# A deformable convolution's sampling weights: two pairs of row positions copied out of PSUM in one operation instead of two

## The chip, the core and the metric

The kernel runs on one core of one Trainium2 chip. The time is device microseconds of the whole program, the median of several runs.

## What is computed

The input `x` is 4 images of 128 channels and 32 x 32 pixels. Two residual blocks follow each other. The first holds nearly all of the instructions that matter here: a 3 x 3 convolution gives, for each pixel and each of nine taps, an offset in y, an offset in x and a mask; each tap reads the image at its shifted, fractional place (four neighbours, bilinear weights), and a 1 x 1 product over taps and channels gives the output.

```python
x = x + L0(group_norm(x))     # deformable 3x3 convolution, bias, group norm of 16 groups
x = x + L1(group_norm(x))     # two ternary 3x3 convolutions with batch norm
...
om = conv2d(x, w_off, b_off)                  # 27 channels
off_y, off_x, m = split(om, 3); mask = sigmoid(m)
py = base_y + kgy + off_y;  px = base_x + kgx + off_x
sampled = sum over 4 corners of x[corner] * wy * wx * valid
sampled = sampled * mask
out = einsum("bckhw,ock->bohw", sampled, weight) + bias
```

## The kernel before

Sampling is done as a matrix product. For a pair of image rows and a half of the columns, the pixels that any tap can reach lie in a window of 6 x 19 = 114 positions. A matrix with 114 rows (positions) and one column for each tap and pixel holds the sampling weights, and TensorE multiplies the window's pixels (`patch`) by it. Products in TensorE's `float32r` form lose low bits, so each operand is split into a high part (`shi`, a rounded copy) and a low part (`slo`, source minus high part).

The work runs over 36 chunks, nine to an image. A chunk n covers two pairs of rows, u = 0 and u = 1, and the ninth of an image only one (`pairs(n)` is 2 in 32 chunks and 1 in 4). The path of the weights of one chunk is:

- GpSimd makes the weights of 128 pixels with the pixels on the partitions (`vt`, L503).
- TensorE turns them: `turn_pairs_out` (L664) writes 16 small transposes, eight taps for each pair, into `S_PAIR[0]` and `S_PAIR[1]`, which are the first two PSUM banks, 114 x 512 numbers each. `turn_last_out` (L673) writes the ninth tap of both pairs into a third bank, `S_LAST`.
- ScalarE copies them to `shi`: `weights_hi`, one copy for each pair (L962) and one for the ninth tap (L966).
- VectorE makes `slo`: `weights_lo`, one subtraction for each pair (L1316), and one for the ninth tap (L1319).
- TensorE samples (`sample`, L693 to L695), into a PSUM area that ScalarE (`vhi`, L974) and VectorE (`vlo`, L1327) empty, and `combine` (L711 to L713) multiplies by the convolution's weights. ScalarE's `output` (L981) empties that.

Each engine runs its own list in a fixed order written by hand, in slots. In slot n TensorE does `sample(n, 0)`, a piece of `combine`, `sample(n, 1)`, then waits for `slo_ok` to reach 3n + 6 (all low parts of chunk n + 1), then does a small job `beside(n)` where there is one, `turn_pairs_out(n + 2)`, another piece and `turn_last_out(n + 2)`. The jobs beside are sums of a normalisation (L552, L557), steps that make the ternary weights (L723, L726, L734) and one test of the offsets (L718). In its slot ScalarE does `sampled_hi(n, 0)`, the hat functions of chunk n + 4 (L953, L955), `output`, `sampled_hi(n, 1)`, `weights_hi(n + 2)` and its own `beside(n)`. VectorE does `sampled_lo(n, 0)`, `sampled_lo(n, 1)`, `weights_lo(n + 2)` and its `beside(n)` (statistics among them, L1216 and L1224). The semaphores `s_mm`, `shi_ok` and `slo_ok` rise by three for each chunk. `turn_pairs_out(n)` also waits for 3n - 1 of `slo_ok`, since it writes over the banks that `weights_lo(n - 1)` reads.

Of the kernel before, what the change touches and what calls it, by code (L numbers as in the profile page):

```python
# [8 lines left out]
ALU = mybir.AluOpType  # L9
ACT = mybir.ActivationFunctionType  # L10
# [3 lines left out]
P = 128  # L14
# [13 lines left out]
KW = WR * WC  # L28
# [25 lines left out]
def build(nc, x, w_off, b_off, wd, bias, gamma, beta, w1, g1, be1, w2, g2, be2, out):  # L54
# [8 lines left out]
    with ExitStack() as ctx:  # L63
        def sb(name, shape, dt=F32, of=None):
            return (of or ctx).enter_context(nc.sbuf_tensor(name, shape, dt))

        def sem(name):
            return ctx.enter_context(nc.semaphore(name))
# [51 lines left out]
        with ExitStack() as own:  # L120
            shi = sb("shi", [KW, 2, TAPS * P], F32R, own)
            slo = sb("slo", [KW, 2, TAPS * P], F32R, own)
# [27 lines left out]
        PS = ctx.enter_context(nc.psum_tensor("PS", [P, 2 * B, BIG], F32))  # L150
# [1 line left out]
        OM_PS = [PS[:, 4 + m, 0:4 * STACK].rearrange("p (j y c) -> p j y c", j=4, y=K) for m in range(4)]  # L152
        T_PS = [PS[:, 2 * m:2 * m + 2, :].rearrange("p a (k c) -> p (a k) c", c=P) for m in range(2)]

        S_PAIR = [PS[0:KW, u, :].rearrange("p (t n) -> p t n", n=P // 2) for u in range(2)]
        S_LAST = PS[0:KW, 2, 0:P]
        WD_PS = [PS[:, m, 0:K * P] for m in (6, 2, 3)]
        V_PS = [PS[:, 3 + 2 * u:5 + 2 * u, 0:2 * TAPS * HALF] for u in range(2)]
# [26 lines left out]
        s_mm, shi_ok, slo_ok = sem("s_mm"), sem("shi_ok"), sem("slo_ok")  # L185
# [74 lines left out]
        def pairs(n):  # L260
            return 1 if n % CH == CH - 1 else 2
# [4 lines left out]
        def pairs_through(n):  # L266
            return pair_no(n, pairs(n) - 1) + 1
# [5 lines left out]
        def taps_at(n, u):  # L273

            s = 4 * (n % CH) + 2 * u
            return (K, TAPS) if s == 0 else (0, 2 * K) if s == H else (0, TAPS)

        def by_pair(m, n):

            return m[:, n % 2, :].rearrange("k (u t p) -> k u t p", u=2, t=TAPS)  # L280

        def first_taps(n):
            return min(TAPS - 1, taps_at(n, pairs(n) - 1)[1])
# [248 lines left out]
        def _(pe):  # L532
# [121 lines left out]
            def turn_pairs_out(n):  # L654
# [6 lines left out]
                for tap in range(first_taps(n)):  # L661
                    for u in range(pairs(n)):
                        at = slice(u * P // 2, (u + 1) * P // 2)
                        ins = t.transpose(S_PAIR[u][:, tap, :], vt[at, n % 2, tap, :], ident[at, at])  # L664
                        if tap == first_taps(n) - 1:
# [220 lines left out]
        def _(act):  # L886
            a = nc.scalar
# [69 lines left out]
            def weights_hi(n):  # L957
                act.wait_ge(s_mm, 3 * n + pairs(n) + (pairs(n) == 1) * 2)
                if n >= 2:
                    act.wait_ge(v_mm, pairs_through(n - 2))  # L960
                for u in range(pairs(n)):
                    a.activation(by_pair(shi, n)[:, u, 0:first_taps(n), :], S_PAIR[u][:, 0:first_taps(n), :],  # L962
                                 ACT.Copy).then_inc(shi_ok, 1 if pairs(n) == 2 else 3)
                if pairs(n) == 2:
                    act.wait_ge(s_mm, 3 * n + 3)
                    a.activation(by_pair(shi, n)[:, :, TAPS - 1, :], S_LAST.rearrange("k (u p) -> k u p", u=2),  # L966
                                 ACT.Copy).then_inc(shi_ok, 1)
# [41 lines left out]
            def slot(n):  # L1009
                if n >= 0:  # L1010
                    sampled_hi(n, 0)
                if n + 4 < CHUNKS:
                    hats(n + 4)
                if ends_in(n):
                    output(*ends_in(n))
                if n in TURNS:
                    copy_weights(TURNS.index(n))
                if n >= 0:
                    sampled_hi(n, 1)
                if n + 2 < CHUNKS:  # L1020
                    weights_hi(n + 2)
                beside(n)
# [125 lines left out]
        def _(dve):  # L1148
            d = nc.vector
# [160 lines left out]
                d.tensor_scalar(fari[0:1, 0:1], far[0:1, B + 1:B + 2], float(REACH), None, ALU.is_le).then_inc(far_ok, 1)  # L1310

            def weights_lo(n):
                for u in range(pairs(n)):
                    dve.wait_ge(shi_ok, 3 * n + (u + 1 if pairs(n) == 2 else 3))
                    src, hi, lo = (m[:, 0:first_taps(n), :] for m in (S_PAIR[u], by_pair(shi, n)[:, u, :, :], by_pair(slo, n)[:, u, :, :]))
                    d.tensor_tensor(lo, src, hi, ALU.subtract).then_inc(slo_ok, 1 if pairs(n) == 2 else 3)  # L1316
                if pairs(n) == 2:
                    dve.wait_ge(shi_ok, 3 * n + 3)
                    d.tensor_tensor(by_pair(slo, n)[:, :, TAPS - 1, :], S_LAST.rearrange("k (u p) -> k u p", u=2),  # L1319
                                    by_pair(shi, n)[:, :, TAPS - 1, :], ALU.subtract).then_inc(slo_ok, 1)  # L1320
# [43 lines left out]
            def slot(n):  # L1364
                if n >= 0:
                    sampled_lo(n, 0)
                    sums_read(n)
                    sampled_lo(n, 1)
                if n + 2 < CHUNKS:
                    weights_lo(n + 2)  # L1370
                beside(n)
# [138 lines left out]
            with dve.Else():  # L1510
# [34 lines left out]
                for b in range(B):  # L1545
# [3 lines left out]
                    with dve.Fori(0, TAPS) as k:  # L1549
# [27 lines left out]
                        for pt in range(NT):  # L1577
                            for half in range(2):
                                n = (it * NT + pt) * 2 + half
# [50 lines left out]
```

## Time and profile before

| | us |
|---|---|
| median of 3 runs (lowest to highest) | 288.46 (288.09 to 289.36) |
| the profiled execution's own time | 288.8 |
| its span, first to last instruction | 287.0 |
| chunks' part of the span | about 38 to 192 |
| PE busy / weight loads busy | 251.6 / 217.6 |
| DVE busy | 193.4 |
| ACT busy | 171.0 |

PE is TensorE, DVE is VectorE, ACT is ScalarE, POOL is GpSimd. The part from 192 us on is the second block's two convolutions, which the change doesn't touch.

### The profile page before, as it was taken

The numbers are of one execution on the slowest core, as the hardware profiler recorded it, in microseconds if no ns is written. First come the engines' busy times: TensorE is split into PE (matmuls) and PEld (weight loads), VectorE is DVE, ScalarE is ACT, GpSimd is POOL, SyncE is SP. The second block draws the span as 40 slices with busy tenths as digits, with TensorE's granted clock in tenths as the row PEclk, the third lists the DMA queues.
The fourth block names the chain that finished last, engine by engine and source line by source line (L and its number), as shares of the span: only waits on it lengthen the run. The fifth ranks groups of instructions, "written<-read, shape, count | busy, mean of one in ns | idle before, by whom it ended". The sixth has DMA issues, their size and how long they took to land.

```text
span 287.0 us, 5560 instructions
## 1 busy us (share of the span) xinstructions
PE 251.6 (88%) x1980; PEld 217.6 (76%) x1980; DVE 193.4 (67%) x450; ACT 171.0 (60%) x366; POOL 136.7 (48%) x193
## 2 busy tenths in 40 slices
PE   2699999999899999989989999999989959999900
PEld 2577667899798899889988889988867737777600
DVE  5689556989888995689977899771365353115194
ACT  2488675888679878788898778830044024330061
POOL 9300799999659688956769875140000000000040
PEclk9999997999999999999999999999999997999965
DMA  7915676544443323333323343000000000000016
GB/s 230 360 36 184 212 256 233 158 134 135 138 136 115 119 64 106 123 95 115 98 83 103 127 129 101 20 2 0 0 0 2 0 0 0 0 3 0 5 40 257
DMA packets 25737, 28.13 MB, mean 98 GB/s; under 512 B 2525, under 2 KB 23629, under 8 KB 25704
## 3 DMA queue, kind: packets, MB, share of 16 engines
q1 hardware_dynamic: 25200, 26.47, 28.1%
q10 hardware_dynamic: 504, 1.24, 1.3%
q8 instruction: 18, 0.29, 0.4%
q14 instruction: 15, 0.12, 0.1%
HBM read 19.87 MB, written 6.78 MB: 93 GB/s over the span
## 4 chain that ended last, share of the span: by engine, by line
PE 65%; DVE 17%; ACT 8%; issue 3%; DMA 3%; POOL 1%; SPq 1%; POOLq 0%; DVEq 0%
PE PS L797 23%; PE PS L711 6%; PE PS L664 5%; PE PS L712 5%; PE PS L713 5%; PE PS L693 5%; PE PS L695 4%; PE PS L694 4%; DVE slo L1316 4%; PE PS L593 3%; ACT vhi L974 3%; DVE vlo L1327 2%; DVE xb L1419 2%; DVE st L1216 2%; ACT shi L962 1%
## 5 line engine op out<-in xcount | busy, mean ns | idle before, releaser
L503 POOL TENSOR_TENSOR vt<-rowm,hat 128x1026 f32<-128x1026 f32 x36 | 70.8, 1966 | 26.0 <-PE PS L673 24.6
L1327 DVE TENSOR_TENSOR vlo<-PS,vhi 128x576 fp32r<-128x576 f32 (+2 forms) x88 | 49.9, 588 | 17.1 <-ACT vhi L974 16.8
L974 ACT ACTIVATE vhi<-PS 128x576 fp32r<-128x576 f32 (+2 forms) x88 | 43.8, 523 | 18.9 <-PE PS L695 18.7
L1316 DVE TENSOR_TENSOR slo<-PS,shi 114x512 fp32r<-114x512 f32 (+1 forms) x68 | 43.2, 674 | 6.4 <-ACT shi L962 6.1
L711 PE MATMUL PS<-vhi,wdhi 128*128 128x256 f32 x144 | 43.8, 304 | 1.8 <-ACT xb L981 1.8
L529 POOL TENSOR_TENSOR xb<-xb,xs 128x512 f32<-128x512 f32 x3 | 3.7, 1278 | 86.0 <-ACT xb L1049 86.0
L693 PE MATMUL PS<-shi,patch 114*128 114x288 f32 (+1 forms) x136 | 43.4, 319 | 0.5 <-DVE omr L1472 0.3
L797 PE MATMUL PS<-xhi,q 128*128 128x512 f32 (+1 forms) x144 | 38.4, 412 | 3.4 <-ACT xhi L1044 3.4
L695 PE MATMUL PS<-shi,patch 114*128 114x288 f32 (+1 forms) x136 | 40.9, 301 | 0.0
L694 PE MATMUL PS<-slo,patch 114*128 114x288 f32 (+1 forms) x136 | 40.8, 300 | 0.0
L713 PE MATMUL PS<-vhi,wdlo 128*128 128x256 f32 x144 | 40.5, 282 | 0.0
L712 PE MATMUL PS<-vlo,wdhi 128*128 128x256 f32 x144 | 40.5, 281 | 0.0
L962 ACT ACTIVATE shi<-PS 114x512 fp32r<-114x512 f32 (+1 forms) x68 | 36.7, 592 | 4.2 <-PE PS L664 3.7
L797 PE MATMUL PS<-xlo,q 128*128 128x512 f32 (+1 forms) x144 | 37.9, 409 | 0.0
L797 PEld LDWEIGHTS PS<-xhi,q 128*128 128x128 f32 x144 | 27.5, 193 | 10.7 <-ACT xhi L1044 3.8
L797 PEld LDWEIGHTS PS<-xlo,q 128*128 128x128 f32 x144 | 27.7, 195 | 6.8
L711 PEld LDWEIGHTS PS<-vhi,wdhi 128*128 128x128 f32 x144 | 27.2, 189 | 4.0 <-issue 1.3
L693 PEld LDWEIGHTS PS<-shi,patch 114*128 114x128 f32 x136 | 26.3, 194 | 1.7 <-issue 1.6
L712 PEld LDWEIGHTS PS<-vlo,wdhi 128*128 128x128 f32 x144 | 27.3, 190 | 0.1
L713 PEld LDWEIGHTS PS<-vhi,wdlo 128*128 128x128 f32 x144 | 27.1, 188 | 0.0
L694 PEld LDWEIGHTS PS<-slo,patch 114*128 114x128 f32 x136 | 26.5, 195 | 0.1
L695 PEld LDWEIGHTS PS<-shi,patch 114*128 114x128 f32 x136 | 26.3, 194 | 0.0
(158 smaller groups left out, 430.9 us busy)
## 6 DMA issues: line engine op xcount, KB each, us to landing
patch<-xt SPq DMA_DIRECT2D x136, 114.0 KB
xt<-xtt SPq DMA_DIRECT2D x4, 1024.0 KB, 6.1
xs<-in_x SPq DMA_DIRECT2D x3, 512.0 KB, 7.7
out<-xb SPq DMA_DIRECT2D x6, 256.0 KB, 2.3
wraw<-in_L_conv_w SPq DMA_DIRECT2D x2, 576.0 KB, 9.8
wd_raw<-in_L_conv_weight ACTq DMA_DIRECT2D x1, 576.0 KB, 6.9
xs<-in_x SPq DMA_DIRECT2D x2, 256.0 KB, 3.9
omr<-omr SPq DMA_DIRECT2D x8, 64.0 KB, 4.1
```

The lines of the kernel that those rows point to most:

```text
L503: g.tensor_tensor(vt[:, n % 2, :, :].rearrange("p t (r j) -> p t r j", r=WR), rowm[:, n % 2, :, :].unsqueeze(3).to_broadcast([P, TAPS, WR, ...
L693: t.matmul(v, patch[:, n % PATCHES, m, 0, :], hi[at], start=True, stop=False)
L694: t.matmul(v, patch[:, n % PATCHES, m, 0, :], lo[at], start=False, stop=False)
L695: last = t.matmul(v, patch[:, n % PATCHES, m, 1, :], hi[at], start=False, stop=True)
L711: t.matmul(O_PS, wdhi[:, w, :], hi, start=(tap == TAPS - 1), stop=False)
L712: t.matmul(O_PS, wdhi[:, w, :], lo, start=False, stop=False)
L713: last = t.matmul(O_PS, wdlo[:, w, :], hi, start=False, stop=(tap == 0))
L797: last = t.matmul(tap_out(PS[:, 2 * b + h, :], h, k), q[:, k, :], tap_in(src, b, h, k), start=(i == 0 and part == 0), stop=(i == TAPS - 1 ...
L962: a.activation(by_pair(shi, n)[:, u, 0:first_taps(n), :], S_PAIR[u][:, 0:first_taps(n), :], ACT.Copy).then_inc(shi_ok, 1 if pairs(n) == 2 ...
L974: last = a.activation(places(vhi), src, ACT.Copy)
L1316: d.tensor_tensor(lo, src, hi, ALU.subtract).then_inc(slo_ok, 1 if pairs(n) == 2 else 3)
L1327: last = d.tensor_tensor(places(vlo), src, places(vhi), ALU.subtract)
```

## The change

The two PSUM banks get one name, `S_PAIRS`, with the pair as a dimension; `S_PAIR[u]` is now a slice of it. `weights_hi(n)` issues one copy over both banks, and `weights_lo(n)` one subtraction over both, with one wait that asks for the whole copy. The counts of the semaphores after each step are as before. The ninth tap's two operations stay, and so do the four chunks with one pair, whose single operation over one bank is the same as before.

```diff
--- before.py
+++ after.py
@@ -152,7 +152,8 @@
         OM_PS = [PS[:, 4 + m, 0:4 * STACK].rearrange("p (j y c) -> p j y c", j=4, y=K) for m in range(4)]
         T_PS = [PS[:, 2 * m:2 * m + 2, :].rearrange("p a (k c) -> p (a k) c", c=P) for m in range(2)]
 
-        S_PAIR = [PS[0:KW, u, :].rearrange("p (t n) -> p t n", n=P // 2) for u in range(2)]
+        S_PAIRS = PS[0:KW, 0:2, :].rearrange("p u (t n) -> p u t n", n=P // 2)
+        S_PAIR = [S_PAIRS[:, u, :, :] for u in range(2)]
         S_LAST = PS[0:KW, 2, 0:P]
         WD_PS = [PS[:, m, 0:K * P] for m in (6, 2, 3)]
         V_PS = [PS[:, 3 + 2 * u:5 + 2 * u, 0:2 * TAPS * HALF] for u in range(2)]
@@ -958,9 +959,8 @@
                 act.wait_ge(s_mm, 3 * n + pairs(n) + (pairs(n) == 1) * 2)
                 if n >= 2:
                     act.wait_ge(v_mm, pairs_through(n - 2))
-                for u in range(pairs(n)):
-                    a.activation(by_pair(shi, n)[:, u, 0:first_taps(n), :], S_PAIR[u][:, 0:first_taps(n), :],
-                                 ACT.Copy).then_inc(shi_ok, 1 if pairs(n) == 2 else 3)
+                a.activation(by_pair(shi, n)[:, 0:pairs(n), 0:first_taps(n), :], S_PAIRS[:, 0:pairs(n), 0:first_taps(n), :],
+                             ACT.Copy).then_inc(shi_ok, 2 if pairs(n) == 2 else 3)
                 if pairs(n) == 2:
                     act.wait_ge(s_mm, 3 * n + 3)
                     a.activation(by_pair(shi, n)[:, :, TAPS - 1, :], S_LAST.rearrange("k (u p) -> k u p", u=2),
@@ -1310,10 +1310,9 @@
                 d.tensor_scalar(fari[0:1, 0:1], far[0:1, B + 1:B + 2], float(REACH), None, ALU.is_le).then_inc(far_ok, 1)
 
             def weights_lo(n):
-                for u in range(pairs(n)):
-                    dve.wait_ge(shi_ok, 3 * n + (u + 1 if pairs(n) == 2 else 3))
-                    src, hi, lo = (m[:, 0:first_taps(n), :] for m in (S_PAIR[u], by_pair(shi, n)[:, u, :, :], by_pair(slo, n)[:, u, :, :]))
-                    d.tensor_tensor(lo, src, hi, ALU.subtract).then_inc(slo_ok, 1 if pairs(n) == 2 else 3)
+                dve.wait_ge(shi_ok, 3 * n + (2 if pairs(n) == 2 else 3))
+                src, hi, lo = (m[:, 0:pairs(n), 0:first_taps(n), :] for m in (S_PAIRS, by_pair(shi, n), by_pair(slo, n)))
+                d.tensor_tensor(lo, src, hi, ALU.subtract).then_inc(slo_ok, 2 if pairs(n) == 2 else 3)
                 if pairs(n) == 2:
                     dve.wait_ge(shi_ok, 3 * n + 3)
                     d.tensor_tensor(by_pair(slo, n)[:, :, TAPS - 1, :], S_LAST.rearrange("k (u p) -> k u p", u=2),
```

ScalarE's list in slot 3, which is `sampled_hi(3, 0)`, the hat functions of chunk 7, `sampled_hi(3, 1)` and `weights_hi(5)`, and the first operation of slot 4, before:

```order
L974 ACTIVATE vhi<-PS 128x2x18x16
L953 ACTIVATE hat<-hat 128x225
L955 ACTIVATE hat<-hat 128x225
L974 ACTIVATE vhi<-PS 128x2x18x16
L962 ACTIVATE shi<-PS 114x512 x2
L966 ACTIVATE shi<-PS 114x2x64
L974 ACTIVATE vhi<-PS 128x2x6x16
```

and now:

```order
L974 ACTIVATE vhi<-PS 128x2x18x16
L954 ACTIVATE hat<-hat 128x225
L956 ACTIVATE hat<-hat 128x225
L974 ACTIVATE vhi<-PS 128x2x18x16
L962 ACTIVATE shi<-PS 114x2x512
L966 ACTIVATE shi<-PS 114x2x64
L974 ACTIVATE vhi<-PS 128x2x6x16
```

Two copies of 114 x 512 became one of 114 x 2 x 512, at the same place in the list; in the changed kernel the hat functions' lines are numbered one higher.

VectorE's list from `weights_lo(2)` to `weights_lo(3)`, with `sampled_lo(1, ...)` between them and the test of the offsets (`far`), before:

```order
L1316 TENSOR_TENSOR slo<-PS,shi 114x512 x2
L1319 TENSOR_TENSOR slo<-PS,shi 114x2x64
L1327 TENSOR_TENSOR vlo<-PS,vhi 128x2x18x16
L1309 TENSOR_REDUCE far<-PS 1x1
L1310 TENSOR_SCALAR fari<-far 1x1
L1327 TENSOR_TENSOR vlo<-PS,vhi 128x2x18x16
L1316 TENSOR_TENSOR slo<-PS,shi 114x512 x2
L1319 TENSOR_TENSOR slo<-PS,shi 114x2x64
```

and now:

```order
L1315 TENSOR_TENSOR slo<-PS,shi 114x2x512
L1318 TENSOR_TENSOR slo<-PS,shi 114x2x64
L1326 TENSOR_TENSOR vlo<-PS,vhi 128x2x18x16
L1309 TENSOR_REDUCE far<-PS 1x1
L1310 TENSOR_SCALAR fari<-far 1x1
L1326 TENSOR_TENSOR vlo<-PS,vhi 128x2x18x16
L1315 TENSOR_TENSOR slo<-PS,shi 114x2x512
L1318 TENSOR_TENSOR slo<-PS,shi 114x2x64
```

Here, too, two operations became one in place and nothing changed its neighbour. TensorE's list holds the same instructions in the same order.

## Rows read from the trace of the kernel before

**Rows 1.** The page's busy times, and its chain that ended last, by engine and line.

```profile
PE 251.6 (88%) x1980; PEld 217.6 (76%) x1980; DVE 193.4 (67%) x450; ACT 171.0 (60%) x366; POOL 136.7 (48%) x193
...
PE 65%; DVE 17%; ACT 8%; issue 3%; DMA 3%; POOL 1%; SPq 1%; POOLq 0%; DVEq 0%
PE PS L797 23%; PE PS L711 6%; PE PS L664 5%; PE PS L712 5%; PE PS L713 5%; PE PS L693 5%; PE PS L695 4%; PE PS L694 4%; DVE slo L1316 4%; PE PS L593 3%; ACT vhi L974 3%; DVE vlo L1327 2%; DVE xb L1419 2%; DVE st L1216 2%; ACT shi L962 1%
```

**Rows 2.** Instructions by line and form: line, operation, tiles, count | busy, mean ns | idle before.

```profile
L1316 DVE TENSOR_TENSOR slo<-PS,shi 114x512 fp32r<-114x512 f32 x64 | 41.0, 682 | 6.4 <-ACT shi L962 6.1
...
L962 ACT ACTIVATE shi<-PS 114x512 fp32r<-114x512 f32 x64 | 34.8, 599 | 4.2 <-PE PS L664 3.7
...
L1467 DVE TENSOR_TENSOR xtt<-PS,xtt 128x1024 fp32r<-128x1024 f32 x4 | 4.9, 1222 | 3.3 <-ACT xtt L943 3.2
...
L943 ACT ACTIVATE xtt<-PS 128x1024 fp32r<-128x1024 f32 x4 | 4.1, 1014 | 0.0
```

**Rows 3.** Timeline of ScalarE and VectorE: start us, us, engine, instruction [idle before it <- releaser].

```profile
51.04 1.09 ACT L962 ACTIVATE shi<-PS 114x512 fp32r<-114x512 f32 x2
51.67 1.29 DVE L1316 TENSOR_TENSOR slo<-PS,shi 114x512 fp32r<-114x512 f32 x2
...
165.41 1.09 ACT L962 ACTIVATE shi<-PS 114x512 fp32r<-114x512 f32 x2 [0.74 <-PE PS L664]
166.04 1.29 DVE L1316 TENSOR_TENSOR slo<-PS,shi 114x512 fp32r<-114x512 f32 x2
...
74.91 1.09 ACT L962 ACTIVATE shi<-PS 114x512 fp32r<-114x512 f32 x2
75.64 1.28 DVE L1316 TENSOR_TENSOR slo<-PS,shi 114x512 fp32r<-114x512 f32 x2
...
47.76 1.08 ACT L962 ACTIVATE shi<-PS 114x512 fp32r<-114x512 f32 x2
48.57 1.28 DVE L1316 TENSOR_TENSOR slo<-PS,shi 114x512 fp32r<-114x512 f32 x2
...
122.78 1.10 ACT L962 ACTIVATE shi<-PS 114x512 fp32r<-114x512 f32 x2
123.60 1.28 DVE L1316 TENSOR_TENSOR slo<-PS,shi 114x512 fp32r<-114x512 f32 x2
```

**Rows 4.** Timeline of TensorE's weight loads at eight places, same columns.

```profile
53.21 0.53 PEld L664 LDWEIGHTS PS<-ident,vt 64*114 64x114 f32 x16 [0.36 <-DVE slo L1319]
...
78.12 0.08 PEld L723 LDWEIGHTS PS<-ident,tw 128*6 128x6 f32 x1 [1.07 <-DVE slo L1319]
...
97.17 0.13 PEld L673 LDWEIGHTS PS<-ident,vt 128*114 128x114 f32 x1 [0.58 <-DVE nsm L1167]
...
116.69 0.42 PEld L734 LDWEIGHTS PS<-ident,wraw 128*128 128x128 f32 x3 [0.51 <-DVE slo L1319]
...
126.63 0.30 PEld L552 LDWEIGHTS PS<-mv,g 128*128 128x128 f32 x2 [1.07 <-issue]
...
129.85 0.30 PEld L557 LDWEIGHTS PS<-nsm,g 128*128 128x128 f32 x2 [0.54 <-DVE slo L1319]
...
134.25 0.33 PEld L552 LDWEIGHTS PS<-mv,g 128*128 128x128 f32 x2
...
156.29 0.19 PEld L711 LDWEIGHTS PS<-vhi,wdhi 128*128 128x128 f32 x1 [0.49 <-issue]
```

**Rows 5.** Timeline of both engines at the widest handover.

```profile
95.95 1.09 ACT L962 ACTIVATE shi<-PS 114x512 fp32r<-114x512 f32 x2
...
97.70 1.28 DVE L1316 TENSOR_TENSOR slo<-PS,shi 114x512 fp32r<-114x512 f32 x2
```

**Rows 6.** Timeline of VectorE just before TensorE's load at 134.25.

```profile
133.65 0.21 DVE L1224 BATCH_NORM_AGGREGATE mv<-st 128x2 f32<-128x12 f32 x1
```

**Rows 7.** Chain that ended last, at one stretch of ScalarE: start us, us, what.

```profile
87.68 0.99 ACT shi L962 x2
```

## The prediction

> **What bounds the kernel now.** I read the page first. TensorE is busy 88% of the span and holds 65% of the chain that ended last, but VectorE holds 17% and ScalarE 8%, and `slo` L1316 alone holds 4% of it, about 11 us [rows 1]. So the change sits on the chain in places, though VectorE is busy only 67% of the time and ScalarE 60% [rows 1]. Neither is short of throughput. What counts is how long after TensorE's transposes the low parts are ready.
>
> Second, the timeline. The reader is to see two things in it. The two copies of a chunk overlap by their ends: each is listed with 599 ns [rows 2], and both together take 1.08 to 1.10 us [rows 3]. And VectorE begins its first subtraction before ScalarE has finished the second copy: at 165.41 the copies begin, at 166.04 the subtractions, 0.63 us later, when the copies have 0.46 us to go [rows 3]. This is a pipeline in two steps: ScalarE is on pair 1 while VectorE is on pair 0. I went through all 32 chunks with two pairs. VectorE starts 0.61 to 0.64 us after ScalarE in twelve, where it waited for the first copy; 0.73 us in five and 0.80 to 0.90 us in eleven, where the `vlo` of the slot ended a little later [rows 3]; and only in four later than 1.06 us, the widest 1.75 us [rows 5], the other three 1.11 to 1.23.
>
> Third, TensorE's waits. Its weight loads show where it stood idle until `slo` or something directly behind it on VectorE was ready [rows 4]: the transposes at 53.21, the ternary sums at 78.12 (two small sums on VectorE come between), the ninth transpose at 97.17 (statistics between), the ternary turn at 116.69, the group sum at 126.63 (statistics between; a second of the same kind at 164.37), and the group squares at 129.85 (a second at 167.58). TensorE fills the rest of a slot with work, and everything behind it on its queue moves with each of these waits.
>
> **The change part by part.** *The prices.* The trace has both new forms nearly as they will be, in other lines: a ScalarE copy out of two PSUM banks, 1024 columns, takes 1.01 us (L943), and a VectorE subtraction of the same size 1.22 us (L1467) [rows 2]. I take these. ScalarE's pair shrinks from 1.09 to 1.01 us, by 0.08, and VectorE's from 1.28 to 1.22, by 0.06. The bounds: at worst nothing is saved (1.09 and 1.28). At best 0.97 and 1.20: these forms have 128 rows and other strides than ours, and I allow 0.04 and 0.02 for it, which is half of the first saving and a third of the second.
>
> *The handover.* In [rows 3] the first subtraction follows the end of the first copy by 0.63 - 0.60 = 0.03 us. Afterwards it can't begin before 1.01 + 0.03 = 1.04 us from the copy's start. A chunk that had handed over after h us has its low parts later by (1.04 - h) - 0.06: 0.35 us for h = 0.63, 0.25 for 0.73, 0.17 for 0.81, and earlier by 0.06 for the four chunks with h over 1.04. So in 28 of 32 chunks the saved instruction makes the result later, since it takes the overlap of the two engines with it.
>
> *Where it is on the path.* Nine handovers stand ahead of the waits named above; [rows 3] has five of them, and the other four repeat their pattern. By time of the copy: 47.76 (h = 0.81, +0.17) and 51.04 (0.63, +0.35) follow each other on the chain to the load at 53.21; the first delays VectorE's test of the offsets and TensorE's transposes, and these the second. 74.91 (0.73, +0.25) to 78.12. The one at 91.66 (0.80, +0.18) to 97.17; its copy itself begins 0.08 earlier, since ScalarE is on the chain just ahead, through another pair of copies [rows 7], which leaves +0.10. The one at 114.34 (0.83, +0.15) to 116.69. 122.78 (0.82, +0.16) to 126.63. The one at 127.68 (0.63, +0.35) to 129.85. The one at 160.61 (0.73, +0.25), and 165.41 (0.63, +0.35), to the second pair of group sums. Sum 0.52 + 0.25 + 0.10 + 0.15 + 0.16 + 0.35 + 0.25 + 0.35 = 2.13 us.
>
> *What is saved.* At two more places ScalarE's pair is on the chain with no subtraction behind it, at 41.2 (ahead of the offsets' last tail) and 144.6 (ahead of a normalisation). Each gives back 0.08: -0.16 us. All other savings are on engines that wait: VectorE's end in idle time ahead of the next `vlo`.
>
> *What hides the rest.* At the other handovers TensorE arrives later than the low parts by 0.4 to 1.7 us, and the delay of at most 0.35 us fits in. The nearest: the mean that the group sum at 134.25 needs ends at 133.86, 0.39 before [rows 4, 6], with a delay of 0.35 on it (h = 0.63); its twin stands at 172. At 155.3 TensorE is met by a delay of 0.25, but then waits 0.49 us for the output's copy at 156.29 anyway [rows 4], and nothing is lost. If that cover were gone, each would cost up to its delay.
>
> The sum is +2.13 - 0.16 = **+1.97 us**. The profiled execution had 288.8 us (span 287.0, and 1.8 around it), which makes 290.8. Its time is 0.3 over the median of the runs; the same +1.97 on 288.46 gives **290.4 us**, 0.7% slower.
>
> The trace shows engines at 60 and 67% whose results TensorE waits for [rows 1, 4]. The Trainium skill, Perfetto Trace Analysis, Optimizing Scalar/DVE Operations, says that grouping helps throughput where the engine is saturated, and that where ScalarE and VectorE aren't saturated but cause bubbles elsewhere, breaking instructions up may finish the work sooner: it speaks against this change. The same section puts the overhead of one VectorE operation on PSUM at about 125 ns, and of a ScalarE one at about 51 ns. By these figures, as an estimate, a low part would come 0.065 us earlier and a copy end 0.03 us later than I have it, and the sum would be near 1.7 us.
>
> **The rivals.**
> *The slack takes most of it* (no measurable change). The places where `slo` is the very last thing waited for, with TensorE idle on it, are 78.12, 116.69, 129.85 and its twin: 0.25 + 0.15 + 0.35 + 0.35 = 1.1 us. The others go through other work (statistics, the test of the offsets, ScalarE's chain), where a later wait, as at 156.29, may have time to give back. The times of idleness there (0.58 at 97.17, 1.07 at 126.63 [rows 4]) speak against that. It would give 288.46 + 1.1 - 0.2 = 289.4.
> *More gates become critical* (slower still). If the prices save nothing, each of the nine handovers costs 0.14 more, and the savings fall away: 1.97 + 9 x 0.14 + 0.16 + 0.08 = 3.5 us, and the covers at 134.25 and its twin, 0.39 us against 0.49, give way by 0.1 each: 3.7 us, 292.2. The forms of [rows 2] speak against it.
> *Fewer instructions win* (faster). VectorE's queue gives back 0.06 us and ScalarE's 0.08 us a chunk. If these engines' throughput set the slot, 32 chunks would give back between 32 x 0.06 = 1.9 and 32 x 0.08 = 2.6 us: 286.2. The point from which it decides is a handover over 1.04 us: VectorE must still be busy when the whole copy is done. That holds in four chunks. It would take another 24 of them to be like [rows 5], and VectorE has idle time in most slots.
> *The change doesn't do what it says*: excluded; the lists show one operation of 2 x 512 in place of two.
>
> **How the numbers follow.** Forecast 0.57, slack takes it 0.27, more gates 0.09, fewer instructions win 0.07. The predicted time is the forecast's. A measurement of this kernel can tell about 0.5% from no change, 1.44 us: from 289.9 on it is slower, under 287.0 faster. The best prices give the forecast 0.06 less at each of the nine handovers, +1.4 us or 289.9, so nearly all of the forecast and the second rival lie beyond the bound, and a part of the first (between 289.4 and the forecast). Slower 0.66, same 0.28, faster 0.06. The range reaches down into the slack's case, to 288.9, and up to the worse prices, 291.9. It leaves out the third rival and the ends of the other two. The forecast's own range is 289.8 to 291.6.
>
> **What the profile after would show.** Right: one copy of about 1.01 us and one subtraction of 1.22 us in a chunk; the subtraction's start 1.04 us after the copy's in about 28 of 32 chunks; VectorE's busy time down by about 32 x (1.36 - 1.22) = 4.5 us by the listed durations, and its waits for `shi` up from 6.1 us [rows 2] by about 12 x 0.41 + 5 x 0.31 + 11 x 0.22 = 8.9 us, to some 15; TensorE's idle time on `slo` up by 0.15 to 0.35 at each load of [rows 4] that I name, and the 192 us mark later by about 2. Wrong: the wider forms cost well over 1.10 or 1.28 us (too low), or TensorE's transposes start as before at 53.21 and 129.85 (too high). The forecast is wrong at the root if the subtraction starts before the whole copy is done, or if the time falls with VectorE's waits for `shi` up.

## The result, and the profile after

The changed kernel takes 292.64 us in the median of four runs (292.51 to 293.53) against 288.27 us for the kernel before. The ratio is 1.0143, with a 95% interval of 1.0116 to 1.0171: 1.4% slower. A second series gave 1.0126 (1.0084 to 1.0169). The direction was forecast, but the 4.4 us are 2.2 times the forecast 1.97 and lie over the range.

The page of the changed kernel, with the lines that answer to [rows 1]:

```profile
PE 252.0 (87%) x1980; PEld 217.5 (75%) x1980; DVE 191.1 (66%) x418; ACT 169.6 (58%) x334; POOL 136.5 (47%) x193
...
PE 65%; DVE 15%; ACT 10%; issue 3%; DMA 3%; SPq 1%; DVEq 0%; ACTq 0%
PE PS L798 23%; PE PS L712 6%; PE PS L665 5%; PE PS L713 5%; PE PS L714 5%; PE PS L694 5%; ACT shi L962 4%; PE PS L696 4%; PE PS L695 4%; DVE slo L1315 4%; PE PS L594 3%; DVE st L1216 2%; DMA xt<-xtt 2%; DVE xb L1418 2%; ACT vhi L974 2%
```

VectorE is busy 2.3 us less and ScalarE 1.4 us less, and the span is 3.8 us longer (290.8 against 287.0). On the chain ScalarE's share rose from 8 to 10%, and its copy L962 from 1 to 4%: now the whole copy, and not just half of it, is waited for. The groups that answer to [rows 2], by form:

```profile
L1315 DVE TENSOR_TENSOR slo<-PS,shi 114x1024 fp32r<-114x1024 f32 x32 | 39.2, 1224 | 17.3 <-ACT shi L962 16.2 <-ACT shi L966 1.0
...
L962 ACT ACTIVATE shi<-PS 114x1024 fp32r<-114x1024 f32 x32 | 32.8, 1026 | 9.2 <-issue 7.0 <-PE PS L665 2.1
```

The new forms cost what the nearest rows had said: 1.03 us for the copy (1.01 taken) and 1.22 us for the subtraction (1.22 taken). But VectorE's idle time ahead of the subtraction rose from 6.4 to 17.3 us, and of ScalarE's 9.2 us ahead of the copy the profile gives 7.0 to "issue", which was not in the row before. Two chunks of the timeline show both, and the first and last transposes bound a stretch:

```profile
50.70 0.53 PEld L665 LDWEIGHTS PS<-ident,vt 64*114 64x114 f32 x16
...
128.76 0.53 PEld L665 LDWEIGHTS PS<-ident,vt 64*114 64x114 f32 x16
...
129.55 1.03 ACT L962 ACTIVATE shi<-PS 114x1024 fp32r<-114x1024 f32 x1 [1.42 <-issue]
...
130.68 1.22 DVE L1315 TENSOR_TENSOR slo<-PS,shi 114x1024 fp32r<-114x1024 f32 x1 [0.66 <-ACT shi L962]
...
132.16 0.30 PEld L558 LDWEIGHTS PS<-nsm,g 128*128 128x128 f32 x2 [1.02 <-DVE slo L1318]
...
168.28 1.03 ACT L962 ACTIVATE shi<-PS 114x1024 fp32r<-114x1024 f32 x1 [1.18 <-issue]
...
169.76 1.23 DVE L1315 TENSOR_TENSOR slo<-PS,shi 114x1024 fp32r<-114x1024 f32 x1 [1.01 <-ACT shi L966]
...
171.23 0.30 PEld L558 LDWEIGHTS PS<-nsm,g 128*128 128x128 f32 x2 [1.37 <-DVE slo L1318]
...
188.54 0.41 PEld L665 LDWEIGHTS PS<-ident,vt 64*114 64x114 f32 x6 [0.17 <-issue]
```

Three things are to be read here. The transposes end at 128.76 + 0.53 = 129.29, and the copy starts at 129.55, 0.26 us later. The copy ends at 130.58, and the subtraction starts at 130.68, 0.10 us later, so the handover is 1.13 us and not 1.04. And at 168.28 it is 1.48: the subtraction starts 0.45 us after the end of its copy. The same rows of the kernel before, at the last of these places and at the ends of the stretch:

```profile
50.30 0.53 PEld L664 LDWEIGHTS PS<-ident,vt 64*114 64x114 f32 x16
...
164.68 0.53 PEld L664 LDWEIGHTS PS<-ident,vt 64*114 64x114 f32 x16
...
167.58 0.30 PEld L557 LDWEIGHTS PS<-nsm,g 128*128 128x128 f32 x2 [0.54 <-DVE slo L1319]
...
184.76 0.41 PEld L664 LDWEIGHTS PS<-ident,vt 64*114 64x114 f32 x6 [0.17 <-issue]
```

Here the transposes end at 165.21, and the copy starts at 165.41 [rows 3], 0.20 us later; the first subtraction had followed its own copy by 0.03.

From the transposes at 50.30 to those at 184.76 the kernel before took 134.46 us, the changed one 188.54 - 50.70 = 137.84. Of the 3.8 us more in the two profiles, 3.38 lie in this stretch and 0.40 ahead of it, and the part behind is alike (102.24 and 102.26 us). The 0.40 can't be put down to the change: in a second profile of each kernel, shown below, the stretch begins at 50.54 before and at 50.42 after. I use this stretch below, since it repeats better than the whole time: the spans of one kernel's runs differ by more than a microsecond, and the last section shows where.

### The profile page after: what moved, and what is told of

It is laid out like the page before. It is cut to its first block, busy times and chain, and to the rows that moved or that the text cites. A ratio compares the mean times of both kernels' runs of the same rounds, so it can differ in the third digit from the quotient of the medians.

```text
span 290.8 us, 5530 instructions
## 1 busy us (share of the span) xinstructions
PE 252.0 (87%) x1980; PEld 217.5 (75%) x1980; DVE 191.1 (66%) x418; ACT 169.6 (58%) x334; POOL 136.5 (47%) x193
## 4 chain that ended last, share of the span: by engine, by line
PE 65%; DVE 15%; ACT 10%; issue 3%; DMA 3%; SPq 1%; DVEq 0%; ACTq 0%
PE PS L798 23%; PE PS L712 6%; PE PS L665 5%; PE PS L713 5%; PE PS L714 5%; PE PS L694 5%; ACT shi L962 4%; PE PS L696 4%; PE PS L695 4%; DVE slo L1315 4%; PE PS L594 3%; DVE st L1216 2%; DMA xt<-xtt 2%; DVE xb L1418 2%; ACT vhi L974 2%
## 5 line engine op out<-in xcount | busy, mean ns | idle before, releaser
L1315 DVE TENSOR_TENSOR slo<-PS,shi 114x1024 fp32r<-114x1024 f32 (+1 forms) x36 | 41.3, 1148 | 17.3 <-ACT shi L962 16.2
L962 ACT ACTIVATE shi<-PS 114x1024 fp32r<-114x1024 f32 (+1 forms) x36 | 34.8, 967 | 9.2 <-issue 7.0
L798 PE MATMUL PS<-xlo,q 128*128 128x512 f32 (+1 forms) x144 | 37.3, 404 | 0.0
```

The source lines that it names most:

```text
L798: last = t.matmul(tap_out(PS[:, 2 * b + h, :], h, k), q[:, k, :], tap_in(src, b, h, k), start=(i == 0 and part == 0), stop=(i == TAPS - 1 ...
L962: a.activation(by_pair(shi, n)[:, 0:pairs(n), 0:first_taps(n), :], S_PAIRS[:, 0:pairs(n), 0:first_taps(n), :], ACT.Copy).then_inc(shi_ok, ...
```

## The experiments

**The kernel before again.** No edit.

> The kernel before, for a second profile of it: from the transposes at 50.30 (chunk 3 of the list) to those at 184.76 (the last chunk) it took 134.46 us, while the spans of equal kernels so far differ by up to 1.5 us in the part behind the chunks and by some tenths in front of them. If this stretch is a sound measure of the chunks, it comes out within 0.3 us of 134.46 again.

```profile
50.54 0.53 PEld L664 LDWEIGHTS PS<-ident,vt 64*114 64x114 f32 x16
...
184.84 0.41 PEld L664 LDWEIGHTS PS<-ident,vt 64*114 64x114 f32 x6 [0.17 <-issue]
```

134.30 us in the stretch: it repeats within 0.16 us. The mean of the two, 134.38, is what the others are compared with. The time of this one run was 288.88 us.

**The change again.** No edit.

> The changed kernel again, as it is. The trace of the first profile has the copy start 0.26 us after the end of TensorE's transposes where it was 0.21, and the subtraction 0.10 after the end of the copy where it was 0.03; and two single late starts (the subtraction at 169.8, 0.45 us behind its copy, and a weight load at 64.0, 0.17 us late). If these belong to the kernel, all four come again in the same places; if the two single ones are chance, they are gone or elsewhere. Time 292.3 to 293.

```profile
50.42 0.53 PEld L665 LDWEIGHTS PS<-ident,vt 64*114 64x114 f32 x16
...
188.22 0.41 PEld L665 LDWEIGHTS PS<-ident,vt 64*114 64x114 f32 x6 [0.17 <-issue]
```

137.80 us in the stretch (137.84 in the first profile), 292.37 us (ratio 1.0126). The lags of 0.26 and 0.10 came again, and so did the late subtraction in the chunk at 168 us, at 1.48 us from the copy. That one belongs to the kernel. So does the late weight load, which comes again at 63.71, 1.60 us after the transposes at 62.11. In the kernel before, and then in the first profile of the changed one:

```profile
63.03 0.19 PEld L693 LDWEIGHTS PS<-shi,patch 114*128 114x128 f32 x1
```

```profile
63.52 0.35 DVE L1326 TENSOR_TENSOR vlo<-PS,vhi 128x192 fp32r<-128x192 f32 x1
...
63.98 0.19 PEld L694 LDWEIGHTS PS<-shi,patch 114*128 114x128 f32 x1
```

Before, the load starts 1.43 us after its transposes (at 61.60), in the changed kernel 1.60 us (after 62.38). It belongs to `sample`, which waits for VectorE's last `vlo` of that PSUM area. That `vlo` now ends at 63.87, 0.11 before the load, and ended at 62.69 before. VectorE's queue has been pushed back behind the later subtraction, and TensorE meets it here.

**Both wait, nothing merged.** The first subtraction asks for both copies:

```diff
-    dve.wait_ge(shi_ok, 3 * n + (u + 1 if pairs(n) == 2 else 3))
+    dve.wait_ge(shi_ok, 3 * n + (2 if pairs(n) == 2 else 3))
```

> The kernel before, with its two copies and two subtractions, but the first subtraction waits for both copies. It takes the overlap of the two engines away and removes no instruction. Theory overlap (the lost overlap is the main cost): the subtraction starts 1.12 us after the copies (1.09 + 0.03) and still takes 1.28, so each of the nine handovers on the path costs (1.12 - h): 0.49 us for h = 0.63, 0.39 for 0.73, 0.31 for 0.81, in sum about 3.4 us, 291.7 to 292.2. Rival (the cost of the change lies in the form of the new operations and not in the overlap): within 0.5 us of the kernel before.

292.26 us, ratio 1.0134 (1.0093 to 1.0174).

```profile
49.51 0.53 PEld L664 LDWEIGHTS PS<-ident,vt 64*114 64x114 f32 x16
...
128.56 1.09 ACT L962 ACTIVATE shi<-PS 114x512 fp32r<-114x512 f32 x2 [1.43 <-PE PS L664]
...
129.68 1.29 DVE L1316 TENSOR_TENSOR slo<-PS,shi 114x512 fp32r<-114x512 f32 x2 [0.60 <-ACT shi L962]
...
187.39 0.41 PEld L664 LDWEIGHTS PS<-ident,vt 64*114 64x114 f32 x6 [0.17 <-issue]
```

The subtraction starts 1.12 us after the copies, as expected, and the stretch takes 137.88 us, 3.5 more than before; the median is just over the expected 291.7 to 292.2. One number in one wait, with the same instructions, costs as much as the whole change, so the rival, which put the cost in the form of the new operations, falls. The lags are the old ones: the copies end at 129.65 and the subtraction starts at 129.68.

**Counting by one.** The copy, and then the subtraction too, raise their semaphores by 1 in the merged kernel. The first edit:

```diff
-    ACT.Copy).then_inc(shi_ok, 2 if pairs(n) == 2 else 3)
+    ACT.Copy).then_inc(shi_ok, 1 if pairs(n) == 2 else 2)
...
-    dve.wait_ge(shi_ok, 3 * n + (2 if pairs(n) == 2 else 3))
+    dve.wait_ge(shi_ok, 2 * n + (1 if pairs(n) == 2 else 2))
```

> The changed kernel, with the copy raising shi_ok by 1 in place of 2 (all waits on it recounted); the subtraction still raises slo_ok by 2. Theory increment (an operation that adds 2 to a semaphore starts 0.05 to 0.07 us later than one that adds 1): the copy starts 0.21 us after the transposes again, and the subtraction, which still adds 2, about 0.08 to 0.10 after the copy; about 0.5 us faster than the changed kernel. Rival form (the shape of 2 x 512 with a gap in its output is slow to start): both lags stay at 0.26 and 0.10, no change of time.

292.74 us, ratio 1.0151 (1.0111 to 1.0191).

```profile
50.37 0.53 PEld L665 LDWEIGHTS PS<-ident,vt 64*114 64x114 f32 x16
...
128.28 0.53 PEld L665 LDWEIGHTS PS<-ident,vt 64*114 64x114 f32 x16
...
129.02 1.03 ACT L962 ACTIVATE shi<-PS 114x1024 fp32r<-114x1024 f32 x1 [1.37 <-PE PS L665]
...
130.15 1.22 DVE L1315 TENSOR_TENSOR slo<-PS,shi 114x1024 fp32r<-114x1024 f32 x1 [0.61 <-ACT shi L962]
...
187.84 0.41 PEld L665 LDWEIGHTS PS<-ident,vt 64*114 64x114 f32 x6 [0.17 <-issue]
```

The copy starts 129.02 - 128.81 = 0.21 us after the transposes, and the subtraction, which still adds 2, 0.10 after the copy. So the lag goes with the operation's own addition and not with that of the one it waits for. The stretch takes 137.47 us, 0.35 less than the changed kernel's 137.82 (mean of two). The whole time shows none of it; the expected 0.5 us is smaller than its noise.

The second edit does the same to `slo_ok`:

```diff
-    d.tensor_tensor(lo, src, hi, ALU.subtract).then_inc(slo_ok, 2 if pairs(n) == 2 else 3)
+    d.tensor_tensor(lo, src, hi, ALU.subtract).then_inc(slo_ok, 1 if pairs(n) == 2 else 2)
```

> The changed kernel, with copy and subtraction both raising their semaphores by 1 (all waits recounted). Theory increment: lags 0.21 and 0.03 as in the kernel before, 0.12 us saved at each of about ten handovers, 1.1 to 1.3 us faster than the changed kernel, so 3.0 to 3.2 us over the kernel before. Rival form: lags 0.26 and 0.10, the changed kernel's time.

290.21 us, ratio 1.0074 (1.0040 to 1.0108).

```profile
50.66 0.53 PEld L665 LDWEIGHTS PS<-ident,vt 64*114 64x114 f32 x16
...
128.22 0.53 PEld L665 LDWEIGHTS PS<-ident,vt 64*114 64x114 f32 x16
...
128.96 1.03 ACT L962 ACTIVATE shi<-PS 114x1024 fp32r<-114x1024 f32 x1 [1.31 <-PE PS L665]
...
130.01 1.23 DVE L1315 TENSOR_TENSOR slo<-PS,shi 114x1024 fp32r<-114x1024 f32 x1 [0.54 <-ACT shi L962]
...
187.06 0.41 PEld L665 LDWEIGHTS PS<-ident,vt 64*114 64x114 f32 x6 [0.17 <-issue]
```

Now the lags are 0.21 and 0.02, the handover 1.05, and the late start near 168 us is gone. The stretch takes 136.40 us, 1.42 less than the changed kernel, where 1.1 to 1.3 were expected. The whole time is 2.2 us under the changed kernel's and 2.1 over the kernel before, where 3.0 to 3.2 were expected; the last section tells why the whole time is the weaker measure here. The operations are the changed kernel's in order, form and duration; only the counts differ.

**Adding two in the kernel before.** Two copies and two subtractions, each adding 2:

```diff
-    ACT.Copy).then_inc(shi_ok, 1 if pairs(n) == 2 else 3)
+    ACT.Copy).then_inc(shi_ok, 2 if pairs(n) == 2 else 5)
...
-    d.tensor_tensor(lo, src, hi, ALU.subtract).then_inc(slo_ok, 1 if pairs(n) == 2 else 3)
+    d.tensor_tensor(lo, src, hi, ALU.subtract).then_inc(slo_ok, 2 if pairs(n) == 2 else 5)
```

> The kernel before, with two copies and two subtractions and their overlap, but each of the four raises its semaphore by 2 in place of 1 (all waits recounted; the single-pair chunks by 5 in place of 3). Theory increment: the copy starts 0.26 us after the transposes in place of 0.21, and the subtraction 0.70 us after the copy in place of 0.63 where it waits; 0.12 us at each of nine handovers, 1.0 to 1.5 us in sum over chunks 3 to 35, and perhaps the late start of 0.35 us at the chunk of 166 us. Rival (what adding 2 costs belongs to the merged form alone): lags as before and no change.

289.12 us, ratio 1.0039 (1.0010 to 1.0068).

```profile
49.74 0.53 PEld L664 LDWEIGHTS PS<-ident,vt 64*114 64x114 f32 x16
...
126.49 0.53 PEld L664 LDWEIGHTS PS<-ident,vt 64*114 64x114 f32 x16
...
127.27 1.08 ACT L962 ACTIVATE shi<-PS 114x512 fp32r<-114x512 f32 x2 [1.18 <-issue]
...
127.97 1.29 DVE L1316 TENSOR_TENSOR slo<-PS,shi 114x512 fp32r<-114x512 f32 x2 [0.23 <-ACT shi L962]
...
184.58 0.41 PEld L664 LDWEIGHTS PS<-ident,vt 64*114 64x114 f32 x6 [0.17 <-issue]
```

Both lags are there without any merging: 127.27 - 127.02 = 0.25, and a handover of 0.70. The rival falls. But the stretch takes 134.84 us, only 0.46 more than before, where I expected 1.0 to 1.5, and the late start doesn't come. (The whole time's interval, 0.3 to 2.0 us, holds both.) The expectation charged 0.12 at each of nine places. That was wrong: the stretch lost 0.11 to 0.12 us at three of them, the waits at 53.21, 129.85 and 167.58, whose handover was 0.63. Where VectorE's `vlo` still held the subtraction back (a handover of 0.73 or 0.8), the lags are hidden behind it in whole or in most part. Adding two costs in full only where each engine waits, and the merging took the chunks in which VectorE waits for the copy from 12 to about 28 of 32.

**Only the copy merged,** counted by 1. The edit is shown against the kernel before; both subtractions now wait for the whole copy:

```diff
-    for u in range(pairs(n)):
-        a.activation(by_pair(shi, n)[:, u, 0:first_taps(n), :], S_PAIR[u][:, 0:first_taps(n), :], ...
+    a.activation(by_pair(shi, n)[:, 0:pairs(n), 0:first_taps(n), :], S_PAIRS[:, 0:pairs(n), 0:first_taps(n), :], ...
```

> Only the copy is merged, raising its semaphore by 1; the subtractions stay two, and both need the whole copy. Theory: the subtraction starts 1.06 us after the copy and takes 1.28, so each handover costs 0.06 more than with both merged and counted by 1; chunks 3 to 35 take 136.8 to 137.1 us (134.46 before, 136.40 with both merged and counted by 1). Rival (most of the loss comes from the subtraction's form, not from the missing overlap): nearer to 134.5 than to 136.4.

292.35 us, ratio 1.0119 (1.0080 to 1.0158).

```profile
50.23 0.53 PEld L665 LDWEIGHTS PS<-ident,vt 64*114 64x114 f32 x16
...
128.84 1.03 ACT L962 ACTIVATE shi<-PS 114x1024 fp32r<-114x1024 f32 x1 [1.37 <-PE PS L665]
...
129.90 1.29 DVE L1316 TENSOR_TENSOR slo<-PS,shi 114x512 fp32r<-114x512 f32 x2 [0.54 <-ACT shi L962]
...
187.25 0.41 PEld L665 LDWEIGHTS PS<-ident,vt 64*114 64x114 f32 x6 [0.17 <-issue]
```

The handover is 1.06 us and the stretch 137.02, within what was expected: 2.64 more than before, so the rival falls. Merging the subtraction too takes 0.62 back (136.40). The merged subtraction was the good half of the change, but it gives back less than a quarter of what the merged copy costs.

**The opposite, more overlap.** TensorE's transposes pair by pair, so that the copy of pair 0 can start after eight:

```diff
-    for tap in range(first_taps(n)):
-        for u in range(pairs(n)):
+    for u in range(pairs(n)):
+        for tap in range(first_taps(n)):
...
-    act.wait_ge(s_mm, 3 * n + pairs(n) + (pairs(n) == 1) * 2)
+    act.wait_ge(s_mm, 3 * n + (1 if pairs(n) == 2 else 3))
...
     for u in range(pairs(n)):
+        if u:
+            act.wait_ge(s_mm, 3 * n + 2)
```

> The opposite of the change, more overlap: the kernel before, with TensorE's sixteen transposes ordered pair by pair in place of tap by tap, and the copy of pair 0 waiting for its eight alone. Theory: the low parts' delay behind TensorE sets the waits; if eight transposes take half of the 0.53 us, the copy starts about 0.27 us earlier where ScalarE is idle, and the waits behind it shrink: up to 1.5 us faster than before. Rival: transposes of one pair behind each other lose what two row groups gave each other, take longer than 0.53 us for sixteen, and TensorE's time grows in each of 36 chunks: slower.

293.28 us, ratio 1.0156 (1.0119 to 1.0194).

```profile
50.80 0.81 PEld L664 LDWEIGHTS PS<-ident,vt 64*114 64x114 f32 x16
...
129.83 0.81 PEld L664 LDWEIGHTS PS<-ident,vt 64*114 64x114 f32 x16
...
130.54 1.09 ACT L964 ACTIVATE shi<-PS 114x512 fp32r<-114x512 f32 x2 [0.80 <-PE PS L664]
...
189.70 0.41 PEld L664 LDWEIGHTS PS<-ident,vt 64*114 64x114 f32 x6 [0.17 <-issue]
```

The sixteen transposes take 0.81 us in place of 0.53, and the stretch 138.90, 4.5 more. The two pairs lie on different partitions of `vt` (0 to 63 and 64 to 127), and taken in turns their transposes may have overlapped; that is argued, only the 0.28 us are shown. The copy at 130.54 does start before the last transpose ends (129.83 + 0.81 = 130.64). But counted from the first transpose it starts after 0.71 us, where it had been 0.53 + 0.21 = 0.74, so ScalarE gains 0.03 and TensorE pays 0.28 in each chunk. Cutting the copies finer, in halves of a bank, wasn't tried: ScalarE and VectorE would then read one PSUM bank at the same time, and no run here shows what comes of that. None of these kernels beats the one before.

## Why the prediction was half right

**Right: the mechanism.** Two engines in a row work as a pipeline, and merging pays in overlap. Waiting for both copies with nothing merged costs 3.5 us by itself. With counts of 1, where my prices hold, the stretch grew by 2.02 us. The prediction's sum for the same stretch is 2.13 less the first handover (0.17, ahead of it) and the 0.08 at 144.6 us: 1.88. Its other estimate, near 1.7, was further off: it took a larger saving on VectorE than came, 0.06 us (1.28 to 1.22).

**Wrong: the step "Afterwards it can't begin before 1.01 + 0.03 = 1.04 us from the copy's start".** It kept the lags of the old operations for the new ones, and took the copy's own start as unmoved. The diff changed `then_inc(..., 1)` into `then_inc(..., 2)` at both, and I read it as bookkeeping. It moved the handover from 1.04 to 1.13 and the copy's start by 0.05. In the stretch that is 137.82 - 136.40 = 1.42 us: 0.35 from the copy, and 1.07 from the subtraction (137.47 - 136.40), of which the late start at 168 us has about 0.35. The sum had no term for it, and the upper bound of the range had neither. With it the forecast would have been 288.5 + 2.0 + 1.4 = 291.9 us, the very top of the range. The median was 292.64. The medians are 4.4 us apart and the stretches 3.4; the 0.9 us between them lies outside the stretch, and no run places it. The ratio's interval (3.3 to 4.9 us) holds 3.4.

**The terms, place by place.** I compare the time between the starts of the transposes around each place with that of the kernel before (first profile), in us; the first number is the prediction's.

| wait (time before) | predicted | counts of 1 | changed kernel |
|---|---|---|---|
| 53.21, second handover | 0.35 | 0.36 | 0.48 |
| 78.12 | 0.25 | 0.00 | 0.01 |
| 63.03, not named | 0 | 0.07 | 0.19 |
| 97.17 (between 86.84 and 95.21) | 0.10 | 0.13 | 0.24 |
| 116.69 | 0.15 | 0.18 | 0.25 |
| 126.63 | 0.16 | 0.19 | 0.25 |
| 129.85 | 0.35 | 0.36 | 0.49 |
| 134.25 | 0 | 0.07 | 0.17 |
| the saving at 144.6 | -0.08 | -0.05 | -0.05 |
| 155.3, with the wait at 156.29 | 0 | -0.01 | -0.02 |
| 164.37 | 0.25 | 0.27 | 0.39 |
| 167.58 | 0.35 | 0.37 | 0.84 |
| twin of 134.25, at 172 | 0 | 0.03 | 0.16 |
| sum | 1.88 | 1.97 | 3.40 |

Against the same profile the whole stretch grew by 1.94 and by 3.38, so the rows account for it. Ten of thirteen are within 0.04 in the kernel whose lags are those I had assumed. In the changed one most are 0.1 higher, the 0.12 of the two lags. The cover at 134.25 (0.39 us against 0.35) gave way, as the worse rival had it. The place at 63.03, the late weight load above, had no term at all. And the term of 97.17 is right in size but not in place: the ninth transpose there stands idle 0.58 us before and 0.59 after, since the delay had come in ahead of it: the group sum's load starts 8.06 us behind the transposes at 86.84 before (at 94.90), and 8.30 behind those at 87.83 after (at 96.13).

**One term was wrong in kind,** the 0.25 at 78.12. VectorE's last small sum there, and GpSimd's product beside it, in the kernel before:

```profile
77.31 0.69 DVE L1250 TENSOR_SCALAR tw<-tw 128x2 f32<-128x2 f32 x1
...
76.01 1.96 POOL L503 TENSOR_TENSOR vt<-rowm,hat 128x1026 f32<-128x1026 f32 x1 [1.86 <-PE PS L673]
```

and in the changed kernel:

```profile
78.70 0.30 DVE L1250 TENSOR_SCALAR tw<-tw 128x2 f32<-128x2 f32 x1
...
77.02 1.96 POOL L504 TENSOR_TENSOR vt<-rowm,hat 128x1026 f32<-128x1026 f32 x1 [1.87 <-PE PS L674]
```

The sum of two elements took 0.69 us before and 0.30 after, and ended both times 0.02 to 0.03 us after GpSimd's product (78.00 after 77.97, 79.00 after 78.98). I had read 78.12 as waiting for `slo`; the sum behind it in fact ended with GpSimd's work, which moves with the transposes and not with `slo`. All ten profiles agree: the sum takes between 0.30 and 0.96 us and always ends 0.02 to 0.03 us after the product. That GpSimd holds it is read from these ends; no run was made to test it, and why it would is open.

**Expected of the profile.** The durations came as written or nearly; the handover came at 1.11 to 1.14 us and not at 1.04, in 28 of 32 chunks. VectorE's busy time fell by 2.3 us and not by 4.5: the listed durations of neighbours overlap, the page counts an overlap once, and 32 x (1.28 - 1.22) = 1.9 us was the figure to take. Its waits for `shi` came to 17.2 us (16.2 and 1.0), 15 expected. TensorE's idle time was to rise by 0.15 to 0.35 at each named load. It did not move at 78.12 and 97.17, and rose by 0.25 to 0.26 at 116.69 and 126.63, by 0.39 at 164.37, by 0.48 at 53.21 and 129.85, and by 0.84 at 167.58.

**The rivals.** "The slack takes most of it" fell at the table above: the waits behind statistics passed the delay on. "Fewer instructions win" fell with the handovers. The two engines stayed unsaturated, and of the rules cited from the Trainium skill (Perfetto Trace Analysis, Optimizing Scalar/DVE Operations) the trace bears out the one on breaking instructions up: two pieces were better than one by 2.0 us even at equal counts. "More gates" gave 292.2 us, the number nearest to the measured one, and that is luck: it rested on forms that save nothing, and they saved what the forecast had said, or nearly (1.03 and 1.22 us against 1.01 and 1.22). The lags took the place of its lost savings.

## What to carry to other kernels

Before merging the pieces that two engines pass to each other, compare the handover with the piece: the second engine began here 0.63 us after the first, and could begin only at 1.04 or later once the piece was whole. An instruction saved on engines busy 60 and 67% of the time was worth 0.06 us, and the lost overlap 0.2 to 0.4. Read every changed number in a diff, semaphore counts too, and recount the waits so that operations on the path add 1.

## What the runs showed of the hardware

An operation that raises its semaphore by 2 starts 0.05 us (ScalarE) to 0.07 us (VectorE) later than one that adds 1. Counted from the end of what it waits for, 0.21 becomes 0.26 on ScalarE and 0.03 becomes 0.10 on VectorE, at nearly every wait of the ten profiles, merged or not. The built programs differ there too: adding 1 is written as an increment, adding 2 as an addition of a number. What in the engine takes the time, no run shows. Nor is it settled why one subtraction of the changed kernel starts 0.45 us after its copy, in three profiles at the same chunk. It doesn't come where VectorE adds 1, and also not in the kernel before with counts of 2, so the count alone doesn't make it.

In all ten profiles the granted clock is 1.00 through the whole stretch. Ahead of it the clock falls in eight of them (0.83 in the mean from 40 to 50 us), and the stretch begins at 50.23 to 50.80 us; in the two where it doesn't fall, it begins at 49.51 and 49.74. The second convolution behind the chunks also runs at a clock that differs between executions, and this is where the whole times of equal stretches part. First the kernel before, then the merged one with counts of 1: a row of its chain, and a window at the beginning of the same convolution (length; busy time of PE, PEld, DVE, ACT, POOL; granted clock; DMA share; GB/s):

```profile
235.98 36.20 PE PS L797 x144
```

```profile
236.00:256.00 20.00, 20.00 (x78) 15.94 (x79) 4.28 (x7) 7.75 (x12) 0.00 (x0) 0.91 0.00 1
```

```profile
238.24 34.73 PE PS L798 x144
```

```profile
238.00:258.00 20.00, 19.76 (x83) 15.75 (x84) 5.24 (x8) 9.22 (x15) 0.00 (x0) 1.00 0.00 1
```

The same 144 products took 36.20 us with a granted clock of 0.91 in that window (a mean between the levels of 2.4 and 1.2 GHz), and 34.73 us at 1.00. So 1.5 us of the 290.21 us against 292.37 may be the clock's, and the counts are shown by the stretch, not by the whole time.
